# Decays of one state of each pair in a PSUM bank, the scan in two instructions, and one bank for the copies of B and C

## What is computed

```
dt = softplus(...); A = -exp(A_log)
dA = exp(dt[:, :, None] * A)                      # decay
dBx = (dt * xc)[:, :, None] * Bm[:, None, :]      # inflow
h = dA_t * h + dBx_t                              # for each node t in turn
y_t = h @ C_t                                     # sum over the 16 states
```

## Time and profile before

| | |
|---|---|
| median of 3 runs | 3835.91 us (3835.72 to 3837.45) |
| the profiled execution's own time | 3837.54 us |
| its span, first to last instruction | 3835.8 us |
| busy: TensorE, VectorE, ScalarE, GpSimd | 2892.4, 2685.3, 2147.8, 2659.7 us |
| middle stage in the profile | 919.5 to 2880 us |

### The profile page before, as it was taken

One profiled execution on the slowest core, in us unless ns is written; L12 is line 12 of the kernel. 1 busy time (PEld: TensorE's weight loads), 2 busy tenths in 40 slices (PEclk: granted clock), 3 DMA queues, 4 the chain that ended last, 5 costly groups with the idle time before them and its releaser, 6 DMA issues. The chain is left out here.

```text
span 3835.8 us, 60997 instructions
## 1 busy us (share of the span) xinstructions
PE 2892.4 (75%) x16306; PEld 2167.6 (57%) x16307; DVE 2685.3 (70%) x4282; ACT 2147.8 (56%) x4790; POOL 2659.7 (69%) x2148
## 2 busy tenths in 40 slices
PE   6465576527788788887887888888883888659998
PEld 5455455415565565565665655655652454448887
DVE  7577566625998888889988888899883788511111
ACT  2322377716777677677676676776772666412222
POOL 2688788877777777777777777777774477424443
PEclk8788767767999999999999999999996999879999
DMA  6433434454444444444444444444456233157665
GB/s 210 114 84 83 134 105 107 116 169 133 122 123 117 125 118 117 126 119 120 122 118 120 123 117 122 119 116 127 119 116 140 51 108 102 68 133 143 143 143 105
DMA packets 291620, 460.16 MB, mean 120 GB/s; under 512 B 55256, under 2 KB 213705, under 8 KB 291113
## 3 DMA queue, kind: packets, MB, share of 16 engines
q0 software_dynamic: 116320, 279.61, 30.7%
q1 hardware_dynamic: 175048, 178.02, 16.0%
HBM read 394.01 MB, written 63.43 MB: 119 GB/s over the span
## 5 line engine op out<-in xcount | busy, mean ns | idle before, releaser
L565 POOL DMA_INDIRECT el_g<-table,el_ix x1344 | 1547.4, 1151 | 407.3 <-issue 394.2
L681 PE MATMUL fl_ps<-el_g,el_oh 128*128 128x260 f32 x3520 | 986.7, 429 | 251.9 <-DVE el_g L608 203.4
L681 PEld LDWEIGHTS fl_ps<-el_g,el_oh 128*128 128x128 f32 x3520 | 715.0, 214 | 371.3 <-DVE el_g L608 210.9
L565 POOL DMA_INDIRECT el_g<-table,eg_src x436 | 590.4, 1354 | 155.9 <-issue 126.7
L608 DVE TENSOR_TENSOR el_g<-el_g,fl_pw 128x1024 f32<-128x1024 f32 x440 | 533.6, 1213 | 17.4 <-ACT fl_pw L652 17.4
L1110 DVE TENSOR_TENSOR_SCAN mb_h<-mb_dA,mb_zero,mb_dB 128x900 f32<-128x900 f32 x224 | 468.1, 2090 | 45.4 <-issue 17.8
L1241 ACT ACTIVATE mb_dA<-mb_dt,mb_a 128x224 f32<-128x224 f32 x900 | 382.8, 475 | 60.3 <-DVE mb_dt L1155 35.4
L1364 PE MATMUL fl_py<-mb_hc,ident 128*128 128x448 f32 x896 | 394.3, 563 | 0.5 <-DVE mb_hc L1120 0.5
L626 ACT ACTIVATE el_away<-el_dst,el_less 128x512 bf16<-128x512 bf16 x445 | 321.1, 722 | 107.5 <-DMA el_dst<-dst_rows 80.4
L641 ACT CAST el_oh<-fl_ptx 128x512 f32<-128x512 bf16 x444 | 253.2, 570 | 214.7 <-PE fl_ptx L668 210.7
L2247 POOL DMA_INDIRECT out<-ex_y,ex_to x112 | 174.1, 1554 | 278.2 <-DVE ex_y L2206 253.5
(11 more groups left out here) (307 smaller groups left out, 5504.0 us busy)
## 6 DMA issues: line engine op xcount, KB each, us to landing
el_dst<-dst_rows SPq DMA_DIRECT2D x446, 128.0 KB, 3.4
ex_w<-in_moe_W SPq DMA_DIRECT2D x56, 512.0 KB, 3.4
el_g<-table,el_ix POOLq DMA_INDIRECT x1344
ex_x<-routed_x SPq DMA_DIRECT2D x56, 257.0 KB, 2.7
el_g<-table,eg_src POOLq DMA_INDIRECT x436
mb_x<-sorted_x SPq DMA_DIRECT2D x30, 224.0 KB
table<-px_tr SPq DMA_DIRECT2D x7, 910.0 KB, 8.2
el_g<-in_x SPq DMA_DIRECT2D x7, 896.0 KB, 7.8
```

The source lines that it names most:

```text
L565: pool.indirect_dma_start(out=G[b // GU][:, b % GU * NJ + j, :], out_offset=None, in_=dram["table"], in_offset=bass.IndirectOffsetOnAxis(a ...
L681: mm = nc.tensor.matmul(pS[n % 2], OH[:, n % (2 * GU), j, :], G[n // GU % 2][:, n % GU * NJ + j, :], start=j == 0, stop=j == NJ - 1)
```

## The change

One of PSUM's banks is given a new use. The copies of B and of C now share the bank `pBC` in turn, and the bank that comes free, `pA`, holds the decays of the first (even) state of each pair; those of the second state stay in SBUF, in two buffers. The scan of a pair becomes two instructions of 450 columns, one that reads its decays from PSUM and one that reads them from SBUF. ScalarE makes the decays of the odd state in the even slot (three slots ahead) and those of the even state in the odd slot (one slot ahead, after the first half of the scan before).

Since one bank serves both copies, `copies_b` now waits for the read-out of the current pair (`hc`) and `copies_c` for the inflow of its pair (`dB`). In TensorE's stream both now come behind `edges_tensor` of their slot, and in an odd slot still ahead of `sum_up`. VectorE's order is as it was.

```diff
@@ -945,7 +945,8 @@
-            pB, pC = ps("fl_pb", [P, 2, TC]), ps("fl_pc", [P, 2, TC])
+            pBC = ps("fl_pbc", [P, 2, TC])
+            pA = ps("fl_pa", [P, 512])[:, 0:1 * KD * (1 + TC)].rearrange("p (s k t) -> p s k t", s=1, k=KD)
             pY, pM = ps("fl_py", [P, KD, TC]), ps("fl_pm", [P, 512])
@@ -1085,6 +1086,7 @@
                 nc.vector.memset(dA[:, :, :, 0:1], 0.0).then_inc(s["set"], 1)
+                nc.vector.memset(pA[:, :, :, 0:1], 0.0).then_inc(s["set"], 1)
...
@@ -1094,7 +1096,7 @@
-                    nc.vector.tensor_tensor(dB[:, :, :, 1:], wide_u, pB[:].unsqueeze(2).to_broadcast([P, 2, KD, TC]), ALU.mult
+                    nc.vector.tensor_tensor(dB[:, :, :, 1:], wide_u, pBC[:].unsqueeze(2).to_broadcast([P, 2, KD, TC]), ALU.mult
                                             ).then_inc(s["dB"], 1)
...
@@ -1106,8 +1108,10 @@
-                    line = lambda t: t.rearrange("p s k t -> p (s k t)")
-                    nc.vector.tensor_tensor_scan(line(H[:]), line(dA[:, n % 2 * 2:n % 2 * 2 + 2]), line(dB[:]), ZERO[:, 0:1],
+                    line = lambda t: t.rearrange("p k t -> p (k t)")
+                    nc.vector.tensor_tensor_scan(line(H[:, 0]), line(pA[:, 0]), line(dB[:, 0]), ZERO[:, 0:1],
+                                                 ALU.mult, ALU.add).then_inc(s["first"], 1)
+                    nc.vector.tensor_tensor_scan(line(H[:, 1]), line(dA[:, n % 2]), line(dB[:, 1]), ZERO[:, 0:1],
                                                  ALU.mult, ALU.add).then_inc(s["h"], 1)
...
@@ -1117,7 +1121,7 @@
-                    nc.vector.tensor_tensor(HC[:, n % 2], H[:, :, :, 1:], pC[:].unsqueeze(2).to_broadcast([P, 2, KD, TC]), ALU.mult
+                    nc.vector.tensor_tensor(HC[:, n % 2], H[:, :, :, 1:], pBC[:].unsqueeze(2).to_broadcast([P, 2, KD, TC]), ALU.mult
                                             ).then_inc(s["hc"], 1)
...
@@ -1234,11 +1238,18 @@
                 def decay(p):
 
                     m, n = p.number, p.n
-                    if not early(m, 4):
-
-                        act.wait_ge(s["h"], two_states(p).number - 1)
+                    if n % 2:
+                        to = dA[:, n // 2 % 2]
+                        if not early(m, 4):
+
+                            act.wait_ge(s["h"], two_states(p).number - 1)
+                    else:
+                        to = pA[:, 0]
+                        if not early(m, 2):
+
+                            act.wait_ge(s["first"], two_states(p).number)
                     for k in range(KD):
-                        ins = nc.scalar.activation(dA[:, n % 4, k, 1:], DT[:, n // NS % 2, k, :], ACT.Exp,
+                        ins = nc.scalar.activation(to[:, k, 1:], DT[:, n // NS % 2, k, :], ACT.Exp,
                                                    scale=A[:, k, n % NS:n % NS + 1])
                     ins.then_inc(s["dA"], 1)
 
@@ -1307,7 +1318,7 @@
                     prepare(c + 1, 1 - b, at)
-                    decay(M + 2)
+                    decay(M + 1 if at % 2 else M + 3)
...
@@ -1337,19 +1348,18 @@
                     if not early(m, 1):
-                        pe.wait_ge(s["dB"], m)
+                        pe.wait_ge(s["hc"], m)
                     for r in range(2):
-                        mm = nc.tensor.matmul(pB[:, r, :], SEL[:, 2 * (n % N2) + r, :], PARTS[:, n // N2 % 2, :],
+                        mm = nc.tensor.matmul(pBC[:, r, :], SEL[:, 2 * (n % N2) + r, :], PARTS[:, n // N2 % 2, :],
                                               start=True, stop=True, skip_group_check=True)
                     mm.then_inc(s["B"], 1)
 
                 def copies_c(p):
 
                     m, n = p.number, p.n
-                    if not early(m, 1):
-                        pe.wait_ge(s["hc"], m)
+                    pe.wait_ge(s["dB"], m + 1)
                     for r in range(2):
-                        mm = nc.tensor.matmul(pC[:, r, :], SEL[:, NS + 2 * (n % N2) + r, :], PARTS[:, n // N2 % 2, :],
+                        mm = nc.tensor.matmul(pBC[:, r, :], SEL[:, NS + 2 * (n % N2) + r, :], PARTS[:, n // N2 % 2, :],
                                               start=True, stop=True, skip_group_check=True)
                     mm.then_inc(s["C"], 1)
 
@@ -1430,12 +1440,12 @@
                     two = two_states(M)
+                    if S:
+                        edges_tensor(pe, S)
                     if at % 2:
                         copies_b(two + 1)
                     else:
                         copies_c(two)
-                    if S:
-                        edges_tensor(pe, S)
                     if at % 2 and not early(M.number, 2):
                         sum_up(two - 1)
```

More of the change, by code:

```diff
@@ L525, in streams @@
         "bx", "bx_hi", "bx_rest", "bx_mid", "bx_mid_sb", "bx_lo", "dt_row", "dt_in", "v", "abs", "e", "ln", "series",
-        "dt", "u", "B", "C", "dA", "dB", "h", "h0", "hc", "y", "skip", "gated", "o", "o_sb", "oT", "oT_sb", "stored")}
+        "dt", "u", "B", "C", "dA", "dB", "h", "first", "h0", "hc", "y", "skip", "gated", "o", "o_sb", "oT", "oT_sb", "stored")}
     gathered = [sem(f"fl_gathered{g}") for g in range(2 * GU)]
@@ L1207, in _ @@
                 nc.vector.memset(dB[:, :, :, 0:1], 0.0).then_inc(s["set"], 1)
-                dve.wait_ge(s["set"], 13)
+                dve.wait_ge(s["set"], 14)
                 run(dve, slot)
@@ L1222, in _ @@
                 nc.scalar.activation(AE[:], A[:], ACT.Exp).then_inc(s["rate"], 1)
-                act.wait_ge(s["set"], 12)
+                act.wait_ge(s["set"], 13)
                 def keep_last(p):
```

## The result

The changed kernel takes 4040.88 us at the median (4034.65 to 4044.89, 4 runs) against 3836.68 us before: 1.0525 times as long, 95% interval 1.0511 to 1.0538, or 204 us more. The forecast was 3963 us, 127 more, with a range that ends at 4032; the direction was right and the size was not. The profiled execution has a span of 4043.1 us. The middle stage, from the first read-out to the last, took 1959 us before and takes 2168 now: the whole difference lies there.

A forecast was written before the change was run, and what follows sets the result against it. VectorE and GpSimd were taken to run at the same pace. Per chunk 1.82 + 2.6 + 7 x 0.06 = 4.84 us, over 28 chunks 135.5, less 8.5: 127 more, 3963 us; range 3905 to 4032.

The forecast's parts named there:

- Two engines at the same pace: Middle stage: GpSimd never stops in 1960.5 us, yet VectorE's own chain would still take some 1940 to 1952 us.
- GpSimd's relief: Gathers beside scans: GpSimd relieved of about 197 us, between nothing and 276; VectorE gets back only 8.5, at most 20.1.
- The prediction's own formula: Gather stall beside a scan of given length: 1.27 us for 2.08 us, 0.35 us for a half of 1.12 us.
- Rival 2: PSUM doesn't free GpSimd, which still needs 1960.5 us: forecast time or 8.5 us more, 3972; 0.1 of the forecast's chance.
- The decays in PSUM: First half of each scan: only the second half can stall gathers; the PSUM input itself costs VectorE nothing.
- The scan in two: Each scan pair on VectorE: two halves cost 0.06 us more, or 0.22 if nothing of a half is hidden.
- The bubble: Between read-out and inflow: 0.54 us in slots 9 and 15, 0.74 in slot 13, 1.82 us a chunk.
- Slots 3 to 5: B's copies behind convolution and edge matmuls: slot 5's inflow at 10.6 us, slot 6's `add` at 11.6; net 2.6 a chunk.
- Elsewhere TensorE has time: Outside slots 3 to 5, from one read-out to the next: TensorE needs 6.2 us, VectorE 7.5, each besides its `prepare`.
- 8.5 us back: VectorE's waits for gathers: 8.5 us, at most 20.1, taken off the forecast as time regained.
- Rival 4: TensorE falls behind after slots 9, 13 and 15, slower after idleness: some 1.0 us each, 4047 us; chance 0.16.
- I add nothing: Behind slot 6's late `add`: scale, logits and what ScalarE derives from them move as a whole, at no further cost.

The follow-up runs named there:

- the last pair of experiments: Kernel before with TensorE's sum of pair 0 and half the convolution moved earlier: with the scan in two 3779.56 us, with the scan in one instruction 3835.4 us.
- the second experiment: Kernel before with only the scan cut in two instructions, all decays in SBUF and all banks as before: 3826.56 us, 0.9983.
- third experiments: The change with a bank each for B and C, TensorE's order as before, and edge weights moved to SBUF: 3890.52 us, 1.0145.

## Why the prediction went wrong in size

*The bottleneck.* Two engines at the same pace was right, and the last pair of experiments shows it from both sides. That GpSimd's relief would come to little in the change was right too: its gathers fell by 143 ns, 192 us in all (197 forecast), and it spent 406 us waiting. What the relief came from was misplaced: most of it is the cut, not PSUM. The prediction's own formula holds this: two halves that both stall would cost 2 x 0.35 = 0.70 us a pair instead of 1.23 (0.56 measured in the second experiment), and PSUM takes away only the first of them (0.38 left in the change). Rival 2, by which GpSimd would need its 1960.5 us still if PSUM didn't help, left the cut out.

*The decays in PSUM.* The first half does not hold gathers up (0.95 us beside it, and none of 166 waited for its end). By the Trainium skill's page SBUF — State Buffer, "Who interferes with whom", that is what one SBUF input means, and the trace agrees. The Trainium skill's page VectorE: DVE Perf Modes (the cycle table under the TRN2 errata) would make the half in PSUM 65 ns dearer, an estimate from its 120 and 58 cycles. The trace doesn't agree: it took 1150 ns, and 1160 with both inputs in SBUF in the second experiment.

*The scan in two.* Forecast 0.06 us a pair, 13 us in all. From the first read-out to the last VectorE's busy time grew by 30 us, but part of that comes from the bubbles, since the 0.08 us that read-out hides behind inflow is lost in each: with the shared bank alone it grew by 8 us, with the cut alone by 17, and from the one to the change by 22. So a pair costs 0.08 to 0.10 us more, and the term was too small by 4 to 9 us.

*The bubble.* Mechanism and size were right at full clock: inflow starts 1.54 us after read-out's start, as forecast, which the profile shows as 0.46 us idle and 0.08 of lost overlap. Slots 9, 13 and 15 waited 37.4 + 18.3 + 15.0 = 70.7 us against 51; 24.5 of the 37.4 is the lower clock in slot 9, and the other 46.2 are 53 with the lost overlap.

*Slots 3 to 5.* Inflow at 10.5 us against 10.6, `add` at 11.8 against 11.6 (11.65 in the mean of 26 chunks). Right.

*The step that failed* is "Elsewhere TensorE has time": 6.2 us of work against VectorE's 7.5 from one read-out to the next. It was added up at full clock. After the waits that the change itself brings, TensorE runs at the 1.2 GHz level, for some 9 us in the chunk shown; from the copies of slot 7 to those of slot 9 it took 9.6 us (2110.39 to 2119.95), and the margin is gone. That cost 24.5 us in slot 9, 28.6 before the give-out in slot 2 and 26.5 before `add` in slot 15: 80 us, against the 77 that were missing. Beside it, the scan's 4 to 9 us, 9 us more at the loop's head and the 20.1 instead of 8.5 us back from the logits' waits nearly cancel. Rival 4 named this mechanism and gave 4047 us, at a chance of 0.16; the rows for it were there (0.56 us instead of 0.36). It looked for the slow work behind the waits of slots 9, 13 and 15. Of these hardly any but slot 13's is followed by it; the other two places are behind slots 1 and 7, so that slot 2 was missed, where `sum_up` is queued behind the wait for the read-out and the give-out waits for the sum. Slot 7 hangs on slots 3 to 6: TensorE's wait there for the turned rows that ScalarE makes late grew from 0.5 to 1.5 us in the mean, ahead of the new 1.2 us for the read-out. The forecast had named what ScalarE derives from the late logits and said "I add nothing"; that was wrong there.

Open: once every 32 slots the scan at the loop's head waits 1.4 to 2.0 us before the change, 2.1 to 2.7 in it, 3.3 to 4.1 with the shared bank alone, and no more than at any other chunk's start (0.2 to 0.4 us) in three kernels with halves and a bank each for B and C: the second and third experiments and that with the halves and the early convolution. Over 12 turns that is up to 40 us, and 16 us of it lie in the gain of the second experiment and in that of the last named. Nothing that was run tells its cause.

## What to carry to other kernels

When a buffer comes to serve two uses in turn, walk the chain from its release to its next use on every engine, and do it twice, the second time with TensorE's work at the lower of its clock levels wherever the new wait lets it idle first. Where one engine's queue never pauses and its consumer hardly waits, both are at the same pace: an edit that relieves only one of them shows little (9 and 0 us here), and they have to be relieved together (57). And before paying a scarce bank for a relief, try the cheaper part of the same edit by itself; here it was a scan cut in two.

## What was not expected of the hardware

A scan of 2.09 us with two SBUF inputs holds up a gather by some 1.2 us, but two of 1.16 and 1.13 us back to back hold gathers up by only (1039 - 946) x 1342 / 224 = 0.56 us a pair in all: 140 of the 200 gathers that started in the first half ended 0.75 us after that half, while the second ran. And four extra matmuls in each of three slots made a kernel 55 us faster: the stage's granted clock rose from 0.90 to 0.97, and the real matmuls behind the waits were slow in fewer chunks.
